# One block of a graph network with experts: four VectorE helpers rewritten, two small operations on ScalarE, expert blocks 16 tiles apart

## The reference

```python
xn = _layernorm(x)                                        # x: (6250, 256)
x = x + gnn(xn, W, b, src, dst) + mix(xn, wq, bq, ...)    # gnn: rows of xn@W+b fetched by src, summed by dst
x = x + ffn(_layernorm(x), gate_w, gate_b, w1, b1, w2, b2)

def ffn(h):                                               # T = 6250 tokens, E = 8 experts, C = 977
    logits = x @ gate_w + gate_b
    probs = softmax(logits)
    idx = argmax(probs); prb = probs[idx]
    pos = number of earlier tokens with the same expert
    kept = pos < C
    hmid = relu(buf[e] @ w1[e] + b1[e])
    ybuf = hmid @ w2[e] + b2[e]
    y = ybuf[idx, pos] * (prb * kept)
    return nan_to_num(y, nan=0.0, posinf=10000.0, neginf=-10000.0)
```

## Time and profile before

| | |
|---|---|
| median of 3 runs | 1551.4 us (1550.78 to 1553.32) |
| profiled execution, its span | 1551.53 us, 1549.8 us |
| busy: TensorE, VectorE, GpSimd, ScalarE | 73%, 59%, 59%, 33% |
| VectorE instructions | 3297 |
| mean granted TensorE clock | 0.875 of full |

### The profile page before, as it was taken

One profiled execution on the slowest core, in us unless ns is written; L12 is line 12 of the kernel. 1 busy time (PEld: TensorE's weight loads), 2 busy tenths in 40 slices (PEclk: granted clock), 3 DMA queues, 4 the chain that ended last, 5 costly groups with the idle time before them and its releaser, 6 DMA issues.

```text
span 1549.8 us, 33330 instructions
## 1 busy us (share of the span) xinstructions
PE 1124.6 (73%) x5569; PEld 762.9 (49%) x5570; DVE 906.8 (59%) x3297; ACT 513.5 (33%) x1355; POOL 918.1 (59%) x966
## 2 busy tenths in 40 slices
PE   2669886445444565787888778887888888887996
PEld 2346553112222233555656556555555555555895
DVE  5854433133333454676667777777777777777564
ACT  2832221011111132343434434444444334444242
POOL 4546777777766776777677766666474456511111
PEclk9999997566666678899999999999899999999898
DMA  7493333444444455455455555555454445423462
GB/s 234 152 261 102 104 104 112 127 133 136 134 132 126 133 167 163 143 177 169 147 174 170 177 159 168 156 153 172 145 173 146 149 150 165 145 94 109 134 191 92
DMA packets 143360, 231.62 MB, mean 149 GB/s; under 512 B 29824, under 2 KB 87329, under 8 KB 143248
## 3 DMA queue, kind: packets, MB, share of 16 engines
q0 software_dynamic: 42896, 115.65, 25.1%
q1 hardware_dynamic: 99118, 114.27, 23.4%
q10 hardware_dynamic: 1234, 0.66, 0.2%
HBM read 197.40 MB, written 35.08 MB: 150 GB/s over the span
## 4 chain that ended last, share of the span: by engine, by line
DVE 29%; issue 27%; POOL 16%; PE 11%; DVEq 9%; ACT 2%; DMA 2%; POOLq 2%; SPq 1%; ACTq 0%
POOL shared L570 16%; DVE shared L1346 4%; PE pY L964 3%; PE pH L973 2%; PE pA L875 2%; DVEq L1301 2%; DVEq L1296 2%; PE pH L855 2%; DVE shared L1466 1%; DVE shared L1464 1%; DMA shared<-table,idx 1%; DVE shared L1455 1%; DVE shared L1469 1%; DVE stats L1387 1%; DVE shared L1463 1%
## 5 line engine op out<-in xcount | busy, mean ns | idle before, releaser
L570 POOL DMA_INDIRECT shared<-table,idx x784 | 765.2, 976 | 312.8 <-issue 274.8
L875 PE MATMUL pA<-shared,onehot 128*128 x976 | 341.5, 470 | 263.2 <-POOLq L550 165.3
L875 PEld LDWEIGHTS pA<-shared,onehot 128*128 x976 | 100.4, 103 | 488.8 <-issue 419.1
L1288 DVE TENSOR_TENSOR onehot<-tile_iota,dst_t 128x512 f32 x244 | 159.8, 695 | 156.3 <-PE pA L875 117.3
L964 PE MATMUL pY<-w2s,shared 128*128 x864 | 203.6, 390 | 5.8 <-issue 4.6
L973 PEld LDWEIGHTS pH<-shared 128*128 128x128 f32 x1728 | 201.4, 192 | 2.7
L973 PE MATMUL pH<-shared 128*128 128x128 f32 x1728 | 201.7, 275 | 0.0
L680 ACT ACTIVATE shared<-pA,rdeg 128x256 f32<-128x256 f32 x49 | 23.2, 473 | 473.3 <-DVE rdeg L1358 473.3
L964 PEld LDWEIGHTS pY<-w2s,shared 128*128 128x128 f32 x864 | 164.0, 195 | 30.0 <-issue 7.3
L730 ACT ACTIVATE shared<-pH,b1s 128x128 f32<-128x128 f32 x432 | 119.8, 376 | 107.9 <-PE pH L973 89.5
L523 POOL DMA_INDIRECT rows<-rows_sb,row_at x49 | 51.6, 1054 | 159.4 <-issue 159.4
(11 more groups left out here) (254 smaller groups left out, 1585.4 us busy)
## 6 DMA issues: line engine op xcount, KB each, us to landing
shared<-in_L_ffn_w_dram SPq DMA_DIRECT2D x108, 512.0 KB, 4.6
shared<-table,idx POOLq DMA_INDIRECT x784
w2s<-in_L_ffn_w_dram SPq DMA_DIRECT2D x8, 1024.0 KB, 6.3
rows<-rows_sb SPq DMA_DIRECT2D x7, 1040.0 KB, 14.7
shared<-rows SPq DMA_DIRECT2D x54, 130.0 KB
shared<-in_L_ffn_b_dram SPq DMA_DIRECT2D x54, 128.0 KB
shared<-in_x_dram SPq DMA_DIRECT2D x12, 512.0 KB, 8.7
table<-w2s SPq DMA_DIRECT2D x12, 512.0 KB, 3.2
```

Of the source, the lines that this page charges most:

```text
L570: g.indirect_dma_start(gathered[:, s * G + j, :], None, table[:, :], bass.IndirectOffsetOnAxis(ap=idx[:, q * G + j:q * G + j + 1], axis=0) ...
L875: m = pe.matmul(pA[:, :], onehot[:, n % OQ, j, :], gathered[:, (f % RQ) * G + j, :], start=False, stop=final and j == G - 1)
L1288: v.tensor_tensor(onehot[:, n % OQ, :, :], tile_iota[:, :].rearrange("p (a n) -> p a n", a=1).broadcast_to([P, G, P]), dst_t[:, bass.ds(ch ...
```

## The change

`route`: 1/std and -mean/std are written where the row needs them, without a copy. The logits are computed with their sign turned, so that the minimum is at once the bias of the exponential, which gets scale -1, and the argmax test becomes "less or equal"; gcon and gbs are negated once in the setup. `place`: expert blocks of the row table are 16 tiles apart, with one tile of empty rows ahead, and the row number is one fused sum; the token numbers come from a table made by GpSimd's iota in the setup and are written by ScalarE. `plan`: each expert's next tile is kept as one number, from which both tile and expert (tile // 16) follow; the highest expert with a full tile is taken, where it was the lowest. `post`: the bias was added and then the whole scaled by the probability; now ScalarE scales the bias in place (`job_bias`) and VectorE does one fused multiply-add; clamping and zeroing NaN are one fused instruction less.

```diff
         def load_plan(eng, j, k):
-            top = NX * SLOTS // P if k == 0 else NX - 1
-            return eng.value_load(planw[0:1, bass.ds(j % PB * 2 + k, 1)], min_val=0, max_val=top)
+            tile = eng.value_load(planw[0:1, bass.ds(j % PB, 1)], min_val=0, max_val=(NX - 1) * ES + JOBS)
+            return tile if k == 0 else eng.snap(tile // ES)
...
             def softmax(t):
                 a.wait_ge(S["nmx_ok"], t + 1)
-                a.activation(lg[:, 1, :], lg[:, 0, :], ACT.Exp, bias=sc[:, 4:5], accum_out=sc[:, 5:6]).then_inc(S["ex_ok"], 1)
+                a.activation(rows_sb[:, t % RB, C_TOK:C_TOK + 1].bitcast(I32), tok_i[:, bass.ds(t, 1)], ACT.Copy)
+                a.activation(lg[:, 1, :], lg[:, 0, :], ACT.Exp, bias=sc[:, 4:5], scale=-1.0, accum_out=sc[:, 5:6]).then_inc(S["ex_ok"], 1)
...
+            def job_bias(j):
+                a.wait_ge(S["b2_in"], j * 16 + 16)
+                a.sem_inc(S["act_hold"], 1)
+                a.activation(b2r, b2r, ACT.Copy, scale=jrow[:, j % JB, C_PRB:C_PRB + 1]).then_inc(S["b2_ok"], 1)
...
                 if inner or 1 <= t <= NT:
                     deviation(t - 1)
+                if out_:
+                    job_bias(t - T0 - 1)
                 if work:
                     hidden(t - T0)
...
             with a.Fori(0, n - 1) as i:
                 job_rows(i + (J0 + 1))
+                job_bias(i + (J0 - 1))
                 hidden(i + J0)
                 columns(i + END, False, True)
             end = a.value_load(last_job, min_val=J0, max_val=J0 + NX * JOBS)
+            job_bias(n + (J0 - 2))
             hidden(end)
+            job_bias(end)
...
                 def route(t):
-                    k(v.reciprocal(rn[:, 0:1], sd[:, 0:1]))
-                    k(v.scalar_tensor_tensor(rn[:, 1:2], sc[:, 0:1], -1.0, rn[:, 0:1], ALU.mult, ALU.mult))
-                    k(v.scalar_tensor_tensor(lg[:, 2, :], gcon[:, 0, :], rn[:, 1:2], gbs[:, :], ALU.mult, ALU.add))
-                    k(v.scalar_tensor_tensor(lg[:, 0, :], lg[:, 4, :], rn[:, 0:1], lg[:, 2, :], ALU.mult, ALU.add))
-                    k.mark(v.tensor_copy(rows_sb[:, t % RB, C_RSTD:C_NMR + 1], rn[:, :]))
-                    k(v.tensor_reduce(sc[:, 3:4], lg[:, 0, :], AX, ALU.max))
-                    v.tensor_scalar(sc[:, 4:5], sc[:, 3:4], -1.0, None, ALU.mult).then_inc(S["nmx_ok"], 1)
-                    k(v.scalar_tensor_tensor(lg[:, 2, :], lg[:, 0, :], sc[:, 3:4], expert_m8[:, :], ALU.is_ge, ALU.mult))
+                    r_std, r_nmr = (rows_sb[:, t % RB, a:a + 1] for a in (C_RSTD, C_NMR))
+                    k(v.reciprocal(r_std, sd[:, 0:1]))
+                    k(v.scalar_tensor_tensor(r_nmr, sc[:, 0:1], -1.0, r_std, ALU.mult, ALU.mult))
+                    k(v.scalar_tensor_tensor(lg[:, 2, :], gcon[:, 0, :], r_nmr, gbs[:, :], ALU.mult, ALU.add))
+                    k(v.scalar_tensor_tensor(lg[:, 0, :], lg[:, 4, :], r_std, lg[:, 2, :], ALU.mult, ALU.add))
+                    v.tensor_reduce(sc[:, 4:5], lg[:, 0, :], AX, ALU.min).then_inc(S["nmx_ok"], 1)
+                    v.wait_ge(S["nmx_ok"], t + 1)
+                    hold(v, "dve_hold")
+                    k(v.scalar_tensor_tensor(lg[:, 2, :], lg[:, 0, :], sc[:, 4:5], expert_m8[:, :], ALU.is_le, ALU.mult))
...
                 def place(t):
-                    k.mark(v.tensor_tensor(cnt16[:, :], cnt16[:, :], oh16[:, :], ALU.add))
-                    k(v.tensor_scalar(sc[:, 8:9], sc[:, 6:7], float(SLOTS), float(NX * SLOTS - 1), ALU.mult, ALU.add))
-                    k.mark(v.tensor_copy(rows_sb[:, t % RB, C_TOK:C_TOK + 1].bitcast(I32), tok[:, :]))
+                    k(v.tensor_tensor(cnt16[:, :], cnt16[:, :], oh16[:, :], ALU.add))
                     k.mark(v.tensor_scalar(sc[:, 9:10], sc[:, 7:8], float(CAP), BIG, ALU.is_gt, ALU.mult))
-                    k(v.tensor_tensor(sc[:, 8:9], sc[:, 8:9], sc[:, 7:8], ALU.add))
-                    k.mark(v.tensor_scalar(tok[:, :], tok[:, :], float(P), None, ALU.add))
-                    k(v.tensor_tensor(row_at[:, bass.ds(t % RB, 1)], sc[:, 8:9], sc[:, 9:10], ALU.add))
-                    v.sem_inc(S["row_ok"], 1)
+                    k(v.scalar_tensor_tensor(sc[:, 8:9], sc[:, 6:7], float(ES * P), sc[:, 7:8], ALU.mult, ALU.add))
+                    v.scalar_tensor_tensor(row_at[:, bass.ds(t % RB, 1)], sc[:, 8:9], float(NX * ES * P + P - 1), sc[:, 9:10],
+                                           ALU.add, ALU.add).then_inc(S["row_ok"], 1)
...
                 def post(j):
-                    v.wait_ge(S["b2_in"], j * 16 + 16)
-                    v.tensor_tensor(y1, pY[:, 0:D], b2r, ALU.add).then_inc(S["y_sb"], 1)
-                    k(v.tensor_scalar(y1, y1, jrow[:, j % JB, C_PRB:C_PRB + 1], None, ALU.mult))
-                    k.mark(v.tensor_scalar(yc, y1, 1.0e4, -1.0e4, ALU.min, ALU.max))
-                    k(v.tensor_tensor(same, y1, y1, ALU.is_equal))
-                    k(v.tensor_tensor(yc, yc, same, ALU.mult))
+                    v.wait_ge(S["b2_ok"], j + 1)
+                    v.scalar_tensor_tensor(y1, pY[:, 0:D], jrow[:, j % JB, C_PRB:C_PRB + 1], b2r, ALU.mult, ALU.add).then_inc(S["y_sb"], 1)
+                    k(v.tensor_scalar(yc, y1, -1.0e4, 1.0e4, ALU.max, ALU.min))
+                    k(v.scalar_tensor_tensor(yc, y1, 0.0, yc, ALU.min, ALU.max))
```

More of the change, by code:

```diff
@@ L49 @@
 JOBS = SLOTS // P
+ES = 16
+ROWS = NX * ES * P
 LO = 2048.0
@@ L77, in gps_block @@
     table = nc.dram_tensor("table", [NT * P, 2 * D], F16).ap()
-    rows = nc.dram_tensor("rows", [NX * SLOTS + P, ROW], F32).ap()
+    rows = nc.dram_tensor("rows", [ROWS, ROW], F32).ap()
     rows_t = rows.rearrange("(s p) d -> s p d", p=P)
@@ L213, in gps_block @@
         cnt16 = sb("cnt16", [P, NX], F16)
-        rn = sb("rn", [P, 2])
         sd = sb("sd", [P, 1])
-        tok = sb("tok", [P, 1])
-        wts = sb("wts", [1, NX + 1])
-        pend = sb("pend", [1, NX + 1])
-        psel = sb("psel", [1, NX + 1])
-        pst = sb("pst", [1, 3, NX + 1])
-        ptmp = sb("ptmp", [1, 2, NX + 1])
-        pout = sb("pout", [1, 4])
+        tok_i = sb("tok_i", [P, NT], I32)
+        first_row = sb("first_row", [1, NX])
+        next_tile_ = sb("next_tile_", [1, NX])
+        pend = sb("pend", [1, 2, NX])
+        pout = sb("pout", [1, 1])
         pA = bank("pA")
@@ L481, in _ @@
             g.wait_ge(S["rows_z"], 2)
-            g.dma_start(rows_t[0:JOBS, :, :].rearrange("s p d -> p s d"),
+            g.dma_start(rows_t[1:1 + JOBS, :, :].rearrange("s p d -> p s d"),
                         empty.rearrange("p (a d) -> p a d", a=1).broadcast_to([P, JOBS, ROW])).then_inc(S["scat_done"], 16)
-            g.dma_start(rows_t[NX * JOBS, :, :], empty).then_inc(S["fin_sc"], 16)
+            g.dma_start(rows_t[0, :, :], empty).then_inc(S["fin_sc"], 16)
             for i in range(BATCHES):
@@ L732, in hidden, with step @@
                     ins.then_inc(S["h_sb"], 1)
-            def step(t, turn=True, work=True):
+            def step(t, turn=True, work=True, out_=True):
                 inner = not isinstance(t, int)
@@ L753, in _ @@
             query(0)
-            step(0, False, False)
+            step(0, False, False, False)
             with a.Fori(1, T0 - 1) as t:
-                step(t, False, False)
-            step(T0 - 1, True, False)
-            with a.Fori(T0, NT - 1) as t:
+                step(t, False, False, False)
+            step(T0 - 1, True, False, False)
+            step(T0, True, True, False)
+            with a.Fori(T0 + 1, NT - 1) as t:
                 step(t)
@@ L1118, in edge_limits @@
                 c(v.tensor_reduce(cmax[:, :], edge_f(0), AX, ALU.max))
-                c.mark(v.tensor_scalar(wts[0:1, :], iota_row[0:1, 0:NX + 1], -1.0, float(NX + 1), ALU.mult, ALU.add))
-                c.mark(v.tensor_scalar(pst[0:1, 1, :], iota_row[0:1, 0:NX + 1], float(JOBS), None, ALU.mult))
-                c.mark(v.tensor_copy(pst[0:1, 2, 0:NX], iota_row[0:1, 0:NX]))
+                c.mark(v.tensor_scalar(first_row[0:1, :], iota_row[0:1, 0:NX], float(ES * P), float(P), ALU.mult, ALU.add))
+                c.mark(v.tensor_scalar(next_tile_[0:1, :], iota_row[0:1, 0:NX], float(ES), 1.0, ALU.mult, ALU.add))
             def edge_columns(a):
@@ L1383, in node_out @@
                     v.tensor_tensor(rows_sb[:, t % RB, 0:D], pX[:, 0:D], tb, ALU.add).then_inc(S["x1_ok"], 1)
-                    k.mark(v.tensor_tensor(lg[:, 4, :], pX[:, D:GW], xgs[:, t, :], ALU.add))
+                    k.mark(v.scalar_tensor_tensor(lg[:, 4, :], pX[:, D:GW], -1.0, xgs[:, t, :], ALU.mult, ALU.subtract))
                     v.wait_ge(S["x1_ok"], t + 1)
@@ L1438, in plan @@
[L1438 to L1442 removed]
+                    k(v.scalar_tensor_tensor(pend[0:1, 0, :], pX[0:1, GW + NX:GW + 2 * NX], float(CAP), first_row[0:1, :], ALU.min, ALU.add))
@@ L1443, in plan @@
+                    k(v.scalar_tensor_tensor(pend[0:1, 0, :], next_tile_[0:1, :], float(-P), pend[0:1, 0, :], ALU.mult, ALU.add))
```

(11 more changed lines are left out.)

33 lines of the change are left out of this document (10 added, 23 removed).

## The result

The changed kernel takes 1489.4 us (median of 4 runs, 1487.2 to 1489.9), the kernel before on the same chip 1551.1 us. The ratio is 0.960, 95% interval 0.958 to 0.962. The profiled execution has a span of 1487.2 us against 1549.8, 62.6 us less. VectorE has 2765 instructions instead of 3297.

What follows compares the result with a forecast made beforehand. VectorE was taken to bind from tile 25, GpSimd's gathers before about 648 us, TensorE in the tail. 50 + 14 + 4 - 2 + 1.6 = 67.6, less 2, from 1551.5 gives 1486 us; range 1473 to 1506.

Steps and rivals of the forecast that it cites:

- The bound: From tile 25 on, VectorE as a single chain sets the pace, 20.14 us per tile falling to 17.95.
- The parts: VectorE per tile: place saves 0.45 us, planner 0.81, router 0.13, job result 0.80, together 2.19; 50 us over tiles 26 to 48.
- The fused form: Two-input fusions 256 wide on VectorE cost 0.42 us, like a plain operation; half throughput would make the sum some 10 us smaller.
- Instructions or waits: On VectorE a small dependent instruction costs 0.19 us, an independent one 0.07, a computed address behind a wait adds 0.10.
- Before tile 11: From the start to tile 11 GpSimd's gathers set the pace, so nothing is gained.
- Tiles 12 to 25: 14 intervals: VectorE alone would give 31 us, GpSimd has 8.5 spare; 14 us taken.
- Rival (d): GpSimd holds the pace beyond tile 25: the 14 us become 8, some tiles more lose half; 1494 us, chance 0.11.
- The tail: From 1454 us TensorE binds; ScalarE scales the late bias before the ReLUs, four done 0.2 us late: nine jobs, 2 us lost.
- The table load: ScalarE's Exp table load (1.28 us), now behind the wait for the router's minimum, is covered and costs nothing.
- Rival (b): TensorE takes over at 19.1 us per tile: 24 us gained, 11 from the other parts; 1516 us, chance 0.08.
- Rival (e): The planner's new choice hands out empty jobs, 7.36 us each; slower from the ninth, ten make 1560 us; chance 0.03.
- The 2 us of friction: 2 us taken off the gain for a step or two where TensorE is held again or a transfer collides.

Runs made afterwards that it cites:

- second trace: The changed kernel itself, with no further edit, run once more on the chip of the two tail variants: 1482.6 us, 0.957.

## Why the prediction was right, point by point

**The bound.** VectorE set the pace from tile 25 on. Shown: of the 2.10 us by which the period fell, 2.08 lie in its own four rewritten parts, TensorE took over only with 1.8 us less, and 1.2 us of GpSimd per tile made no difference there. But it was a near thing, and luck helped. The forecast had TensorE's unheld round at 18.1 us, above its own 17.95 for VectorE, and let VectorE bind all the same. Its waiting of 1.06 us per tile for L1364 came from one tile, too; it is 10.7 us in 15 of the 23. Unheld, TensorE needs 17.25 us in the mean (four instructions left out, granted clock 1.00, where the forecast's rows had 0.94), so the 18.1 was too high. Before, TensorE's sum had ended 5.3 to 7.9 us ahead of VectorE's L1355; in the changed kernel it's 1.2 to 5.9 us, and in its second trace 0.15 us in one tile.

**The parts.** In the mean of the 23 tiles place saved 0.49 (forecast 0.45), planner 0.77 (0.81), and the job result, from its first instruction to the next tile, 0.81 (0.80). The router saved 0.12 up to its test (L1397 to L1404 1.46 us, L1407 to L1414 1.34; forecast 0.13). But from its last instruction to the job result's first, 0.41 us became 0.52, and that goes with the job result: it is 0.41 in both kernels that have the old one with the new place part and planner, whichever the router, and 0.52 in the kernel before with the new job result alone. The forecast had nothing there. L1457 reads the probability at a computed address, which may be the reason; no run changes that alone. Together 2.10 us, the same in tiles with three groups and with four, for 2.19: 48.3 us for 50. That the one tile above shows exactly 2.19 is chance. From kernel to kernel the 2.10 split in another way, and the means account for it: place part and planner have 1.45, 1.25 of their own and 0.2 in parts nobody edited; the job result has 0.62 to 0.63, 0.7 less 0.1 at its start; the router has 0.01, since 0.09 of its 0.12 were there without it.

**The fused form.** L1462 takes 0.43 us with two f32 sources in SBUF, the duration of a plain two-input operation before. A job result that is 0.81 us cheaper shows no penalty either. So the trace doesn't bear out the half throughput that the Trainium skill gives for it ("Vector Engine (DVE) Microarchitecture Reference", Points that are easy to get wrong).

**Instructions or waits.** The router lost two instructions and 0.12 us up to its test, where one wait was added, the planner lost three and 0.77 us, since each of these was a dependent step. The advice of the Trainium skill to count instructions and not semaphores ("VectorE: DVE Perf Modes", Rules for kernel authors) would, at 0.15 us an instruction, give the router 0.30 and the planner 0.45; the trace goes with the waits.

**Before tile 11: the step that failed.** I had nothing there, since the gathers bind. But GpSimd issues them itself and waits for VectorE's row numbers in between, before tile 11 as after it: between 259.5 and 647.9 us of the trace before, 8.9 us in 8 events, of which the changed kernel has 5.2. The forecast took that view only from tile 11 on. The start of tile 11 is at 647.3 and 647.9 in the two traces without the new place part and planner, and between 636.0 and 642.3 in the eleven with them that scatter; counted from tile 0, it is 388.4 and 388.6 against 379.2 to 383.9 us. The waits account for 3.7 of the 8.2 us; 2.4 are there at tile 0 already, which may be setup or chance; the other 2 are open.

**Tiles 12 to 25.** 14 was too much. The spare time of 8.5 us was the ceiling, and the wait shrank by little. 5.0 came (294.4 in the second trace, 5.2). The two errors cancel, which is luck: at tile 25 the forecast had 14 and the trace 13.2. Rival (d) was right in this stretch and wrong beyond it.

**The tail.** The mechanism was right, the term mis-sized: 3.5 us instead of 2. The ReLUs that I had 0.2 us late per job hold TensorE for 0.44 to 0.71 us in every second one (both traces). It belongs to the scaling alone, since it comes and goes with it (76.1 to 77.4 us in the six traces that scale the bias there with its issue where it was, 72.9 to 73.1 in the three that don't).

**The rest.** The table load was covered, as costed. Rival (b), TensorE at 19.1, was wrong: TensorE's wait for L1364 is gone, and the idle time before L895 (L908 after) fell from 21.0 us in 23 tiles to 4.8 us in 10. Its 11 us from the other parts have no working; the forecast's own terms for them add up to 17.6. Rival (e) didn't happen, there are 54 jobs. The 2 us of friction were not seen as such.

## What to carry to other kernels

Price an edit on a chained engine by the dependent steps and computed addresses that it takes out, not by its instructions, and check each stretch for who waits for that engine, also where another one seems to bind. Take a term from the mean of many tiles, not from one. Work that is moved to an idle engine takes over its waits: put it ahead of what the bottleneck wants and a late transfer comes with it, put it behind and the loop through a single buffer closes. Before such a move, write down the loop that the moved result stands in, and compare it with the period.
